# Token-table stores moved between the weight loads, one order of weight homes, and the output stored from two queues, in a macaron block (experts, attention, experts) on one core

## The reference

```python
x = x + 0.5 * _L0_ffn_ref(_layernorm(x), router_w, w1, v1, w2)
x = x + _L0_attn_ref(_layernorm(x), Wq, bq, Wk, bk, Wv, bv, Wo, bo)
x = x + 0.5 * _L0_ffn_ref(_layernorm(x), router_w, w1, v1, w2)

# the experts: E = 64, of which each row of T takes K = 8; F = 96, at most C = 32 rows an expert
logits = x @ router_w.T
probs = softmax(logits); wts, idx = top_k(probs, K); wts = wts / sum(wts)
xg = rows of x gathered by expert, at most C each, in token order
h = silu(einsum('ecd,efd->ecf', xg, w1)) * einsum('ecd,efd->ecf', xg, v1)
y = einsum('ecf,efd->ecd', h, w2)
out = scatter-add of y * weight to the tokens

# the attention: 16 heads of 128 in 4 groups of keys and values, S = 256
Q = (x @ Wq + bq); K = (x @ Wk + bk); V = (x @ Wv + bv)
attn = softmax(Q K^T / sqrt(128)); out = (attn V) @ Wo + bo
```

## Time and profile before

| | |
|---|---|
| median of three runs | 716.96 us (715.67 to 717.71) |
| the profiled execution | 716.03 us, span 714.2 us |
| PE busy, share of the span | 622.6 us, 87% |
| DVE, ACT, POOL busy | 517.9, 373.9, 52.5 us |
| mean granted clock of TensorE | 0.946 |
| moved by DMA | 62.50 MB |
| the chain that ended last, by engine | PE 80%, DVE 11%, ACT 4%, issue 2%, DMA 2% |

### The profile page before, as it was taken

One profiled execution on the slowest core, in us unless ns is written; L12 is line 12 of the kernel. 1 busy time (PEld: TensorE's weight loads), 2 busy tenths in 40 slices (PEclk: granted clock), 3 DMA queues, 4 the chain that ended last, 5 costly groups with the idle time before them and its releaser, 6 DMA issues.

```text
span 714.2 us, 11936 instructions
## 1 busy us (share of the span) xinstructions
PE 622.6 (87%) x4498; PEld 525.1 (74%) x4498; DVE 517.9 (73%) x1307; ACT 373.9 (52%) x1002; POOL 52.5 (7%) x55
## 2 busy tenths in 40 slices
PE   3626995899999999999999999999999998664995
PEld 1313764699998979999897999898899996331774
DVE  6773656789987778778777777876878776875542
ACT  1402454577665656666555656665566665331442
POOL 3124300000000000000000000000000000124310
PEclk9957996999999999999999999999999999886998
DMA  9995950000000000000000000000000052793921
GB/s 329 423 395 165 351 221 1 0 1 1 1 1 2 1 1 0 2 1 1 1 1 1 1 1 1 1 1 0 1 1 1 1 207 89 309 397 90 387 65 46
DMA packets 27229, 62.50 MB, mean 88 GB/s; under 512 B 6880, under 2 KB 17248, under 8 KB 26912
## 3 DMA queue, kind: packets, MB, share of 16 engines
q1 hardware_dynamic: 25600, 56.45, 20.8%
q0 software_dynamic: 1568, 5.25, 2.3%
HBM read 54.34 MB, written 7.34 MB: 86 GB/s over the span
## 4 chain that ended last, share of the span: by engine, by line
PE 80%; DVE 11%; ACT 4%; issue 2%; DMA 2%; POOL 0%; SPq 0%; DVEq 0%; ACTq 0%
PE bank L1162 19%; PE bank L1164 18%; PE bank L1163 18%; PE bank L1214 8%; PE bank L1021 4%; PE bank L1053 4%; PE bank L1063 2%; PE bank L1096 2%; PE bank L992 2%; DVE best L754 1%; DVE ln L676 1%; DVE keys L756 1%; PE bank L1010 1%; DMA slots<-token_table,slot_index 1%; DVE stats L664 1%
## 5 line engine op out<-in xcount | busy, mean ns | idle before, releaser
L590 ACT ACTIVATE probs<-bank,negmax 128x256 f32<-128x256 f32 x256 | 121.4, 493 | 0.0
L603 ACT CAST probsT_hi<-bank 128x512 fp32r<-128x512 f32 x128 | 68.9, 590 | 80.5 <-PE bank L1214 80.5
L936 DVE TENSOR_TENSOR probsT_lo<-bank,probsT_hi 128x512 fp32r<-128x512 f32 x128 | 82.0, 681 | 1.4 <-ACT probsT_hi L603 1.4
L904 DVE TENSOR_REDUCE negmax<-bank 128x2 f32<-128x512 f32 x128 | 81.9, 681 | 0.7 <-PE bank L1164 0.7
L573 ACT ACTIVATE o_hi<-bank,bv 128x512 fp32r<-128x512 f32 x64 | 44.2, 690 | 64.6 <-PE bank L1164 64.6
L912 DVE TENSOR_SCALAR probs<-probs,rowinv 128x256 f32<-128x256 f32 x256 | 73.1, 350 | 2.3
L1162 PE MATMUL bank<-k_hi,q_hi 128*128 128x256 f32 x256 | 72.5, 283 | 2.5 <-DVE q_lo L890 2.5
L1162 PE MATMUL bank<-o_hi,wo_hi 128*128 128x256 f32 x256 | 73.1, 286 | 1.6 <-DVE o_lo L890 1.6
L890 DVE SCALAR_TENSOR_TENSOR o_lo<-bank,bv,o_hi 128x512 fp32r<-128x512 f32 x64 | 48.0, 751 | 36.0 <-ACT o_hi L573 36.0
L1164 PE MATMUL bank<-o_hi,wo_lo 128*128 128x256 f32 x256 | 72.5, 283 | 0.0
L1164 PE MATMUL bank<-k_hi,q_lo 128*128 128x256 f32 x256 | 72.5, 283 | 0.0
(11 more groups left out here) (162 smaller groups left out, 1318.5 us busy)
## 6 DMA issues: line engine op xcount, KB each, us to landing
up_r<-up_in SPq DMA_DIRECT2D x12, 768.0 KB, 8.3
up_q<-up_in SPq DMA_DIRECT2D x12, 768.0 KB, 9.0
down_r<-down_in SPq DMA_DIRECT2D x11, 512.0 KB, 9.1
down_q<-down_in SPq DMA_DIRECT2D x11, 512.0 KB, 11.5
up_o<-up_in SPq DMA_DIRECT2D x6, 768.0 KB, 17.8
token_table<-xn SPq DMA_DIRECT2D x16, 256.0 KB, 10.1
down_o<-down_in SPq DMA_DIRECT2D x6, 512.0 KB, 17.7
x<-x_in SPq DMA_DIRECT2D x4, 512.0 KB, 5.6
```

The source lines that it names most:

```text
L590: nc.scalar.activation(probs[:, n % 2, t, :], scores_ps[head][:, qt * S:qt * S + S], ACT.Exp, bias=negmax[:, n % 2, t:t + 1], accum_out=ro ...
L603: nc.scalar.copy(probsT[0][:, head].rearrange("p c s -> p (c s)"), probsT_ps[head][:]).then_inc(probsT_high, 1)
L904: nc.vector.reduce_max(negmax[:, n % 2, 2 * head:2 * head + 2], scores_ps[head][:].rearrange("p (t s) -> p t s", t=2), AX.X, negate=True). ...
L936: nc.vector.tensor_tensor(probsT[1][:, head].rearrange("p c s -> p (c s)"), probsT_ps[head][:], probsT[0][:, head].rearrange("p c s -> p ( ...
```

## The change

Three things are changed.

1. One order of homes for both layers: q, r, o, s, r. In layer 0 the first four groups now use q, so wk, wq and wv wait for the fourth group and not the eighth; the last four loads of both layers wait for groups 5 to 8; the wait for the fourth gather is gone.
2. In layer 0 the table's stores stand between the loads: five loads, four stores of xn, one load, four stores of xn, four loads, the two stores of expw, two loads. wk, wq and wv now stand ahead of the last four loads. In layer 1 the order of stores and loads is as before, but for the homes.
3. At the end PE adds bank 5 first, then 6 and 7. DVE copies bank 5 and then bank 7, ACT copies bank 6. ACT issues the stores of bank 6 and half of those of bank 5 itself; SP issues the other half of bank 5 and then bank 7.

```diff
+        place_of_group = homes_q + homes_r + homes_o + homes_s + homes_r
...
-            for g in range(AHEAD):
-                load(0, g)
-            expert_layer(0)
+            def load_when_free(layer, g):
+
+                earlier = [n for n in range(g) if home(layer, n) is home(layer, g)]
+                sp.wait_ge(down_done, GROUPS * layer + earlier[-1] + 1)
+                load(layer, g)
+
+            for g in range(5):
+                load(0, g)
+            store_tokens(0)
+            store_tokens(1)
+            load(0, 5)
+            store_tokens(2)
+            store_tokens(3)
+            for g in range(6, 10):
+                load(0, g)
+            store_weights()
+            for g in range(10, AHEAD):
+                load(0, g)
 
             sp.wait_ge(down_done, done_with_q)
             sp.dma_start(wk_raw[:], wk_in.rearrange("(k p) n -> p k n", p=P)).then_inc(wk_loaded, 16)
...
+            for g in range(AHEAD, GROUPS):
+                load_when_free(0, g)
             sp.wait_ge(down_done, done_with_o)
...
             sp.dma_start(result[0, rows:P], x[rows:P, 0:TILES:2, :]).then_inc(out_stored, 16)
-            for n in range(2):
-                sp.wait_ge(staged[n], 1)
-                for odd in range(2):
...
             sp.wait_ge(staged[2], 1)
-            for j in range(4):
...
+            for j in range(2):
+                store_narrow(sp, j)
+            sp.wait_ge(staged[1], 1)
+            for odd in range(2):
+                store_wide(sp, 1, odd)
...
                 if layer == 1:
-                    act.wait_ge(bank_summed, 2 + 1)
+                    act.wait_ge(bank_summed, 2 + 2)
                     nc.scalar.copy(stage[:, 0, :], bank[6][:]).then_inc(staged[0], 1)
-                    act.wait_ge(bank_summed, 2 + 3)
-                    nc.scalar.copy(stage[:, 2, :], bank[5][:]).then_inc(staged[2], 1)
+                    act.wait_ge(staged[0], 1)
+                    for odd in range(2):
+                        store_wide(nc.scalar, 0, odd)
+                    act.wait_ge(staged[2], 1)
+                    for j in range(2, 4):
+                        store_narrow(nc.scalar, j)
...
-                    dve.wait_ge(bank_summed, 2 + 2)
+                    dve.wait_ge(bank_summed, 2 + 1)
+                    nc.vector.tensor_copy(stage[:, 2, :], bank[5][:]).then_inc(staged[2], 1)
+                    dve.wait_ge(bank_summed, 2 + 3)
                     nc.vector.tensor_copy(stage[:, 1, :], bank[7][:]).then_inc(staged[1], 1)
```

More of the change, by code:

```diff
@@ L268, in macaron_kernel @@
         attention_done = sem("attention_done")
-        layer_homes = [homes_r + homes_q + homes_o + homes_s + homes_r,
-                       homes_q + homes_r + homes_s + homes_o + homes_q]
+        place_of_group = homes_q + homes_r + homes_o + homes_s + homes_r
         AHEAD = GROUPS - 4
-        done_with_q = layer_homes[0].index(homes_q[-1]) + 1
-        done_with_o = layer_homes[0].index(homes_o[-1]) + 1
+        done_with_q = place_of_group.index(homes_q[-1]) + 1
+        done_with_o = place_of_group.index(homes_o[-1]) + 1
         def home(layer, g):
-            return layer_homes[layer][g]
+            return place_of_group[g]
         def loads_before(layer, g):
@@ L331, in fills, with store_wide, store_narrow @@
             return more
+        result = out.rearrange("(b h p) d -> h p b d", h=2, p=P)
+        rows = FIRST[1] // B
+        def store_wide(engine, n, odd):
+            engine.dma_start(result[0, 0:WIDE, 4 * n + odd:4 * n + odd + 3:2, :],
+                             stage[WIDE * odd:WIDE * odd + WIDE, n, :].rearrange("p (b d) -> p b d", b=2)).then_inc(out_stored, 16)
+        def store_narrow(engine, j):
+            engine.dma_start(result[0, WIDE:rows, j:B:4, :],
+                             stage[NARROW * j:NARROW * j + NARROW, 2, :].rearrange("p (b d) -> p b d", b=2)).then_inc(out_stored, 16)
         block = ctx.enter_context(nc.Block())
@@ L341, in _ @@
                 sp.dma_start(dst[:], src).then_inc(small_loaded, 16)
-            xn_seen, weights_seen, downs_seen = Tally(xn_ready), Tally(weights_ready), Tally(down_done)
+            xn_seen, weights_seen = Tally(xn_ready), Tally(weights_ready)
             def load(layer, g):
@@ L349, in load @@
                 sp.dma_start(down_home[0:rows], down_in[g * F:g * F + rows, :].rearrange("f (j d) -> f j d", j=EG)).then_inc(loaded, 16)
[L351 to L358, removed]
+            rows_of_table = table[0:T, :].rearrange("(h p b) e -> h p b e", h=2, p=P)
@@ L359, in expert_layer, with store_tokens, store_weights @@
+            def store_tokens(n):
+                sp.wait_ge(xn_ready, xn_seen.add(4))
+                for half in range(2):
+                    sp.dma_start(rows_of_table[half, :, 2 * n:2 * n + 2, 0:D],
+                                 xn[:, 4 * n + half:4 * n + half + 3:2, :]).then_inc(table_written, 16)
+            def store_weights():
                 sp.wait_ge(weights_ready, weights_seen.add())
                 for half in range(2):
-                    sp.dma_start(rows[half, :, :, D:ROW],
+                    sp.dma_start(rows_of_table[half, :, :, D:ROW],
@@ L394, in _ @@
                 load(1, g)
-            expert_layer(1)
+            for n in range(4):
+                store_tokens(n)
+            store_weights()
+            for g in range(AHEAD, GROUPS):
+                load_when_free(1, g)
             sp.wait_ge(limit_ready, 2)
@@ L400, in _ @@
                 sp.wait_ge(late_added[1], RANGES)
-            result = out.rearrange("(b h p) d -> h p b d", h=2, p=P)
             sp.dma_start(result[1], x[:, 1:TILES:2, :]).then_inc(out_stored, 16)
-            rows = FIRST[1] // B
             sp.dma_start(result[0, rows:P], x[rows:P, 0:TILES:2, :]).then_inc(out_stored, 16)
-            for n in range(2):
-                sp.wait_ge(staged[n], 1)
-                for odd in range(2):
-                    sp.dma_start(result[0, 0:WIDE, 4 * n + odd:4 * n + odd + 3:2, :],
-                                 stage[WIDE * odd:WIDE * odd + WIDE, n, :].rearrange("p (b d) -> p b d", b=2)).then_inc(out_stored, 16)
-            sp.wait_ge(staged[2], 1)
-            for j in range(4):
-                sp.dma_start(result[0, WIDE:rows, j:B:4, :],
-                             stage[NARROW * j:NARROW * j + NARROW, 2, :].rearrange("p (b d) -> p b d", b=2)).then_inc(out_stored, 16)
+            sp.wait_ge(staged[2], 1)
+            for j in range(2):
[3 more added lines that the diff above has]
+                store_wide(sp, 1, odd)
             sp.wait_ge(out_stored, 16 * 10)
@@ L1001, in sum_slots @@
                 marks = onehot[:, s % MARKS, :]
[L1002 to L1006, removed]
                 if layer == 1:
@@ L1011, in sum_slots @@
                                       y_parts[:, s, low, :], start=False, stop=final and low == 1, skip_group_check=True)
+                    if final:
+                        last.then_inc(bank_summed, 1)
+                for n in range(2):
+                    for low in range(2):
+                        last = sum_wide(bank[6:8], n, marks, y_parts[:, s, low, :], False, final and low == 1)
                     if final:
```

## The result

The changed kernel takes 713.9 us, the median of six runs (713.03 to 714.14), the kernel before 717.17 in the same comparison (six runs, 715.67 to 717.71). The ratio is 0.9955, with a 95% interval from 0.9945 to 0.9966: 3.3 us faster (2.4 to 3.9), where 6.5 were forecast. The profiled execution took 714.14 us with a span of 712.3.

What follows compares the result with a forecast made beforehand. DMA order was taken to tell only in the two expert layers, with layer 0's late gathers and the end's store issuing as targets. Gains of 4.1 and 2.4 make 6.5 us: 716.96 to 710.5 us, range 708.5 to 712.

Steps and rivals of the forecast that it cites:

- the term of 4.1 us: Layer 0: with stores between the loads, the second gather lands 4.1 us earlier and all behind it moves ahead.
- The first gather at 50.0: Layer 0: the first gather starts at 50.0 instead of 56.20, a gain of 6.2 us at that place.
- The second gather at 56.3: Layer 0: the second gather, which TensorE waits for, lands at 56.3 instead of 60.43, a gain of 4.1 us.
- keeps all: Rival, chance 0.12: loads hardly hinder layer 0's gathers, so 6.2 and 2.4 make 8.6 us gained, 708.4 us.
- the 6.5 of rows 7: Layer 0 before: the other ten gathers, most beside loads, landed in 4.0 to 8.0 us, 6.5 in the middle.
- The clock: Layer 0: TensorE's granted clock, 0.50 while waiting, rises from the lower level in both kernels; the 4.1 us stay.
- The order of homes: Both expert layers: homes of q first delay the last four loads, with nothing gained and nothing lost.
- The spare of 4.9 us: Layer 0: the last load is in at 91.0 and wanted at 95.9, so it is hidden with 4.9 us to spare.
- The danger I had given 0.05: Rival, chance 0.05: layer 0's last four loads come late behind wk, wq and wv; 3.8 us slower at 225 GB/s, 720.8.
- The end: Kernel's end: narrow sums first and stores from two queues gain 2.4 us, taken between 2.6 and 1.9.
- my 8.3 us before: Kernel's end: time from the first copy to the end of the span in the kernel before, 8.3 us.
- The estimate of 1.9: Kernel's end: if 200 GB/s is the DMA engines' limit, 0.79 MB take 3.9 us, a gain of 1.9 us.

Runs made afterwards that it cites:

- the half alone: The changed kernel with the old end, so only the order of homes and the stores between the loads: 714.96 us, ratio 0.9962 to the kernel before.
- the kernel that holds two loads: The changed kernel, but loads 10 and 11 of layer 0 issued only when the second gather has landed: 712.25 us, ratio 0.9922 to the kernel before.
- with four loads held: The changed kernel with eight loads ahead of the weights' store and four held until the second gather has landed: 713.32 us, ratio 0.9941 to the kernel before.
- with five: The changed kernel with eight loads ahead of the weights' store and four held until the fifth gather: 716.55 us, ratio 0.997 to the kernel before.
- the kernel with the transposes: 68 unread transposes in each expert layer, added to the kernel holding four loads until the fifth gather: 720.73 us, ratio 1.003 to the kernel before.

## Why the prediction was right or wrong

- **Layer 0, the term of 4.1 us.** Its mechanism was right: the stall named "issue" was the table's store behind two loads too many, and it shrank from 6.63 to 2.08 us. But this is the term that failed: the half alone gives 2.7 (1.8 to 3.6). By the forecast the first up matmul would start at 57.1 (61.22 less 4.1); it started at 59.43, and at 58.38 in the half's profile. Two steps of the working were wrong, and a third cost a little.
- **The first gather at 50.0** was the first step that failed. I counted bytes on the mean of the DMA engines. By bytes the sum nearly holds: the loads were out at 46.0, where I had 45.7, and most of the store by 48. But its last bytes came until about 50, at a DMA share of 0.13, and the gather waited for them. The kernels with ten loads ahead start it at 51.51, 50.73, 51.13 and 50.21, those with an empty queue at 49.84, 49.33 and 49.34, as soon as the indices are there: 0.4 to 1.8 us late.
- **The second gather at 56.3** was the second; it landed at 58.0. I let it finish a little under 2 us behind the loads' end at 54.5. But the loads themselves began 1 to 2 us later (between 49 and 50 instead of at 48), after SP had been held 2.68 us at the first of them, and with them all moved. The first gather, which I had taken to be out of the way, took 6.04 us, and TensorE waited for that one, until 57.59. Holding the loads gave 2.91. The rival "keeps all" was wrong. The Trainium skill's rule of taking turns ("DMA: Bandwidth & Descriptors", "Queues, rings and completion order") was no ground for it: it says in what order an engine serves its queues, and the gather still took twice as long here, 6.04 against 2.91 us. That lies near the 6.5 of rows 7, which I had discounted.
- **The clock.** I wrote that it has to rise in both and that all behind moves ahead by the full amount. In the profiled execution 1.1 us went at its rise. Over the executions of the half alone 2.7 us arrived, about what the first up matmul showed (1.8 and 2.8 us ahead in two profiles). So the 1.1 us look like scatter and not like a loss in every execution; no run here separates the two.
- **The order of homes** costs and gains nothing by itself: right (0.9995). The spare of 4.9 us was wrong: 0.2 us of wait in one profile and 1.2 in the other show that there was none, and this is the third loss of layer 0. The loads did move at about the rate that I had taken (10.2 MB in 27.3 us, 374 GB/s), but I had counted only 8.26 MB. The seven gathers of that stretch moved 1.15 MB beside them, and 0.8 MB of wo, behind the last load in SP's queue, had moved before that load was complete. These 1.9 MB are 5 us at 385 GB/s, all of the spare. The danger I had given 0.05, loads too late behind wk, wq and wv, is the one that took back 4 us and more in two of the experiments.
- **The end**: 1.4 us (0.8 to 2.0) alone and 1.9 in the profiles, against 2.4. The term's mechanism was right and its size was not. First, the issues were longer: in the changed kernel's profile 0.7 to 0.9 us for each narrow store instead of 0.52, and in all profiles of the new end with whole stores 2.6 to 3.5 us for the four stores of one engine instead of 2.4. Second, my 8.3 us before held the one slow issue of 1.64 us: the old end takes 7.8 to 8.3 us in three profiles, the new one 6.3 to 6.8 in eight. The estimate of 1.9 from 0.79 MB at 200 GB/s met the number, but the engines then moved 250 and 265 GB/s, so not by its reason. The Trainium skill's sentence that a second issuing engine saves only the sequencer's time ("DMA: Bandwidth & Descriptors", "Issuing engines are not separate DMA queues") agrees with the runs in what it saves: eight stores took 5.3 us to issue on one engine and 3.2 on two. That this is usually small beside the DMA does not hold for this end, as 1.0005 with one queue and 0.998 with two show.

Together 2.7 and 1.4 make 4.1 against 3.3 (2.4 to 3.9) measured for both, which the intervals allow.

## What to carry to other kernels

When a small store or gather is late behind bulk loads, moving it ahead in the queue is half the work: what is issued right behind it will meet the next small transfer, so hold the bulk back until that has landed. Count the time of a queue to its last bytes and not to the mean of the DMA engines, and count everything that shares the engines, gathers and the next load in the queue included, before calling a load hidden. And after each gain look for the load with the next deadline: here the same early start was worth 2 us or 8 depending on whether four loads stood behind or ahead of weights that nobody wanted yet.

## What the runs showed of the hardware that I had not expected

- Two stores, 0.52 MB together in rows of 256 bytes, moved their bytes in about 2 us on an empty queue (46 to 48, with eight loads ahead). Behind the rest of a queue of loads they took about 4 us (46 to 50): with nothing issued behind them, in the kernel that holds two loads, 33 and 17 GB/s moved in the last two us, at a DMA share of 0.15 and 0.08.
- A gather of 128 rows takes 2.9 us on free DMA engines and 5.8 to 6.0 with bulk loads on the same engines, though on a queue of its own.
- ScalarE issues a plain store as fast as SP, 0.7 us, and the four of one queue run beside the four of the other.
- The granted clock, up at 1.00 from 49 to 55 through otherwise useless transposes, was back at 0.50 for the first groups.
- After a wait of about 2 us on a load near the loop's end the granted clock fell to 0.50 in two profiles (98 to 100 with four loads held, 102 to 104 with five), and the loop's rest took 1.5 us longer or more. Not every late load did this: in the kernel with the transposes and in layer 0's half the clock stayed at 1.00 until the loop's end.
